# Position bias at block distances 2, 4 and 8 as one shape over summed spike blocks, in a spiking attention and expert kernel

## The reference, cut

```python
Q, K, V = (lif(layer_norm(query @ W.T + b, g, beta), 1.0) for each)   # spikes, 16 heads of 16
hamming = q_sum + swapaxes(k_sum) - 2.0 * qk
attn = Dh - hamming + log_pe_bias(N, N)      # max(ceil(log2((N-1) / (|i-j|+1))), 0)
out = lif(einsum('bhlm,bhmd->bhld', attn * scale, V), 0.5)
out = lif(layer_norm(out @ Wo.T + bo, go, betao), 1.0)
x = x + out + experts(xn)
```

## Time and profile before

| | |
|---|---|
| median of 3 runs | 443.77 us (443.08 to 443.96) |
| the profiled execution | 444.79 us, its span 442.9 us |
| busy | PE 378.5 (85%), DVE 273.0 (62%), ACT 232.5 (52%), POOL 214.5 (48%) |
| L1300 bias matmuls | 114, busy 380 ns each (pipelined) |
| L699 and L692 on POOL | 16 of 1332 ns and 11 of 1314 ns |
| y_tok loads | 8 of 1024 KB, 14.1 us to landing |

### The profile page before, as it was taken

How to read it: one execution, slowest core, us unless ns; L and a number is a source line. 1 busy time by engine, 2 the same in 40 slices (tenths; PEclk the granted TensorE clock), 3 DMA queues, 4 the chain that set the end, 5 groups by cost and what they waited for, 6 DMA issues and landing times.

```text
span 442.9 us, 9338 instructions
## 1 busy us (share of the span) xinstructions
PE 378.5 (85%) x2521; PEld 306.0 (69%) x2522; DVE 273.0 (62%) x774; ACT 232.5 (52%) x752; POOL 214.5 (48%) x213
## 2 busy tenths in 40 slices
PE   5388958999999508999999999999999998999840
PEld 1223657999999506778888888888888875666630
DVE  5796899777778505454445545444554434479994
ACT  1436835888888504544455455445445434466650
POOL 5215336777777750333333333333333332489993
PEclk9796979999999956999999999999999999999995
DMA  8880063424222231533334334333334413982222
GB/s 256 257 285 1 10 228 101 174 91 150 95 101 103 95 109 48 169 118 122 119 125 124 119 119 130 120 122 126 121 119 121 115 61 109 382 319 96 95 73 95
DMA packets 40108, 58.93 MB, mean 133 GB/s; under 512 B 5974, under 2 KB 27606, under 8 KB 40088
## 3 DMA queue, kind: packets, MB, share of 16 engines
q1 hardware_dynamic: 31392, 38.53, 27.6%
q0 software_dynamic: 6848, 18.70, 11.6%
q10 hardware_dynamic: 1848, 1.47, 1.1%
HBM read 35.79 MB, written 22.89 MB: 132 GB/s over the span
## 4 chain that ended last, share of the span: by engine, by line
PE 41%; POOL 26%; issue 13%; DMA 6%; DVE 5%; ACT 4%; SPq 3%; DVEq 0%; POOLq 0%; ACTq 0%
POOL slot_x L658 14%; PE bank L1085 12%; PE bank L1087 11%; PE bank L1086 11%; POOL xres L699 4%; POOL xres L692 3%; SPq L309 3%; PE bank L1212 3%; PE bank L1228 3%; DMA ew_f<-experts 2%; DMA vec_d<-two_col 2%; DVE exT_l L910 2%; POOL slot_x L665 2%; ACT gact L519 2%; DMA ex<-slot_x 1%
## 5 line engine op out<-in xcount | busy, mean ns | idle before, releaser
L673 POOL DMA_INDIRECT slot_y<-ey,dest x71 | 68.5, 965 | 139.7 <-ACT ey L535 111.4
L973 DVE TENSOR_TENSOR hid<-gact,bank 128x256 f32<-128x256 f32 x71 | 29.9, 421 | 77.6 <-ACT gact L519 77.6
L658 POOL DMA_INDIRECT slot_x<-xn,pos x64 | 64.7, 1011 | 25.6 <-issue 19.2
L1085 PE MATMUL bank<-ew,exT_h 128*128 x142 | 63.6, 448 | 5.3 <-DVE exT_l L910 5.2
L519 ACT ACTIVATE gact<-bank 128x256 f32<-128x256 f32 x71 | 27.4, 386 | 65.7 <-PE bank L1087 65.7
L1087 PE MATMUL bank<-ew,exT_l 128*128 x142 | 56.9, 401 | 0.0
L1086 PE MATMUL bank<-ew,exT_h 128*128 x142 | 56.8, 400 | 0.0
L1085 PE MATMUL bank<-w_h,xT_h 128*128 128x256 f32 x192 | 54.3, 283 | 0.0
L1087 PE MATMUL bank<-w_h,xT_l 128*128 128x256 f32 x192 | 54.1, 282 | 0.0
L1086 PE MATMUL bank<-w_l,xT_h 128*128 128x256 f32 x192 | 54.1, 282 | 0.0
L1085 PE MATMUL bank<-ew,hidT_h 128*128 x142 | 45.7, 322 | 1.0 <-DVE hidT_l L977 1.0
(11 more groups left out here) (183 smaller groups left out, 967.4 us busy)
## 6 DMA issues: line engine op xcount, KB each, us to landing
ex<-slot_x SPq DMA_DIRECT2D x71, 129.0 KB, 2.0
y_tok<-slot_y SPq DMA_DIRECT2D x8, 1024.0 KB, 14.1
xres<-x SPq DMA_DIRECT2D x16, 256.0 KB, 2.7
out<-xres SPq DMA_DIRECT2D x16, 256.0 KB, 2.1
xn<-x SPq DMA_DIRECT2D x6, 512.0 KB, 11.7
ew_f<-experts SPq DMA_DIRECT2D x1, 2560.0 KB, 10.1
ew_f<-experts SPq DMA_DIRECT2D x1, 2048.0 KB, 10.3
slot_y<-ey,dest POOLq DMA_INDIRECT x71, 2.4
```

The source lines that it names most:

```text
L658: pool.indirect_dma_start(slot_x, bass.IndirectOffsetOnAxis(ap=pos[:, k, t:t + 1], axis=0), xn[:, t, :], None).then_inc(s["scattered"], 16)
L673: pool.indirect_dma_start(slot_y, bass.IndirectOffsetOnAxis(ap=dest[:, m % 4:m % 4 + 1], axis=0), ey[:, m % 4, :], None).then_inc(y_out[m ...
L973: v.tensor_tensor(hid[:, m % 2, :], gact[:, m % 2, :], h_ps[m % 2][:, F:2 * F], ALU.mult).then_inc(s["hid_done"], 1)
L1085: mm(dst, a_h, b_h, start=first, stop=False)
```

## The change

OFFSETS, the distances with a matmul and a table of their own, shrink to 0, 1 and -1. For distances 2, 4 and 8 to one side the tables differ by a constant only. So the spikes of the three blocks are summed first, one matmul takes the common shape (UP for one side, DOWN for the other) times the sum, and the constants go to the far matmul's map. DVE makes the sums: `pair_v[a]` = block a + block a+2 for 14 values of a inside the expert loop, and `triple_v` = a pair and a single, one for each block a in the last stage, two slots. (The pair a+2 with a+4, and a+8; or on the other side a-4 with a-2, and a-8.) A side with two blocks takes a pair, with one block the spikes.

With it: output spikes `spk` become 16 bit and lie over `qT`, whose rows the same block has used. kv's correction has a place of its own, `less`. The first eight blocks of x (`xres_a`) are loaded in the expert loop, over `xn`, beside the pairs; the other eight (`xres_b`) behind the first two quarters of `y_tok`, at the end of the experts' weights. DVE waits for the scatter before its first pair.

```diff
-OFFSETS = [0, 1, -1, 2, -2, 4, -4, 8, -8]
+OFFSETS = [0, 1, -1]
+STEPS = [2, 4, 8]
+UP, DOWN = len(OFFSETS), len(OFFSETS) + 1
+PAIRS = NB - 2
+EARLY_RES = NB // 2
...
+        put = place_in(r_x)
+        xres_a = put("xres_a", [P, EARLY_RES, B, D])
+        pair_v = put("pair_v", [P, PAIRS * B * D], BF16)
+        triple_v = put("triple_v", [P, 2, B * D], BF16)
...
+        xres_b = put("xres_b", [P, NB - EARLY_RES, B, D])
+        less = put("less", [P, B * KC, P])
...
+        spk = place_in(r_q)("spk", [P, NB, B, D], BF16)
...
-            with sp.Fori(0, QUADS - 2) as i:
-                sp.dma_start(xres[:, bass.ds(i * B, B), :], x_pairs[:, bass.ds(i, 1), :, :].rearrange("p a b d -> p (a b) d")).then_inc(s["xres_in"], 16)
+            with sp.Fori(0, EARLY_RES) as i:
+                sp.dma_start(entry(xres_a, i), x_pairs[:, bass.ds(i, 1), :, :].rearrange("p a b d -> p (a b) d")).then_inc(s["xres_in"], 16)
+                for u in range(4):
+                    load_tile(i * 4 + (8 + u), u)
+            with sp.Fori(EARLY_RES, QUADS - 2) as i:
                 for u in range(4):
                     load_tile(i * 4 + (8 + u), u)
...
+                if c in (1, 2):
+                    half = (NB - EARLY_RES) // 2
+                    lo = (c - 1) * half
+                    for b in range(B):
+                        sp.dma_start(xres_b[:, lo:lo + half, b, :], x_pairs[:, EARLY_RES + lo:EARLY_RES + lo + half, b, :]).then_inc(s["xres_late"], 16)
...
                 if a == 0:
-                    pool.wait_ge(s["xres_in"], 16 * NB)
+                    pool.wait_ge(s["xres_in"], 16 * EARLY_RES)
+                if a >= EARLY_RES and a % 4 == 0:
+                    pool.wait_ge(s["xres_late"], 16 * B * (1 + (a - EARLY_RES) // 4))
...
+            def add_pair(a):
+
+                v.tensor_tensor(cut(pair_v, a * B * D, B * D), cut(v_spk, a * B * D, B * D), cut(v_spk, (a + 2) * B * D, B * D),
+                                ALU.add).then_inc(s["pair_set"], 1)
+
+            dve.wait_ge(s["spk_done"], G3 * NT)
+            dve.wait_ge(s["scattered"], 16 * TOPK * NT)
+            with dve.Fori(1, PAIRS + 1) as i:
+                for u in range(4):
+                    expert(i * 4 + u, 4 + u, i)
+                    if u == 1:
+                        add_pair(i - 1)
+            with dve.Fori(PAIRS + 1, QUADS) as i:
                 for u in range(4):
                     expert(i * 4 + u, 4 + u, i)
...
+            def add_triple(a):
+
+                if a == 0:
+                    dve.wait_ge(s["pair_set"], PAIRS)
+                if a >= 2:
+                    dve.wait_ge(s["s_done"], a - 1)
+                pair, single = (a + 2, a + 8) if a + 8 < NB else (a - 4, a - 8)
+                v.tensor_tensor(triple_v[:, a % 2, :], pair_v[:, pair * B * D:(pair + 1) * B * D],
+                                v_spk[:, single * B * D:(single + 1) * B * D], ALU.add).then_inc(s["triple_set"], 1)
...
+            add_triple(0)
+            add_triple(1)
             for a in range(NB + 2):
                 if a < NB:
                     out_spike(a)
+                if a + 2 < NB:
+                    add_triple(a + 2)
                 if a >= 2:
                     out_variance(a - 2)
...
+                if a == 0:
+                    pe.wait_ge(s["pair_set"], PAIRS)
+                pe.wait_ge(s["triple_set"], a + 1)
+                for way, shape in ((1, UP), (-1, DOWN)):
+                    if 0 <= a + 2 * way < NB:
+                        mm(dst[:, :], toep_s[:, shape, :], v_sum(a, way), start=False, stop=False, skip_group_check=True)
                 mm(dst[:, :], far_s[:, a * P:(a + 1) * P], far_v[:, :], start=False, stop=False, skip_group_check=True)
```

More of the change, by code:

```diff
@@ L131, in spiking_moe @@
         xn = place_in(r_x)("xn", [P, NT, ROW])
-        xres = place_in(r_x)("xres", [P, NT, D])
+        put = place_in(r_x)
+        xres_a = put("xres_a", [P, EARLY_RES, B, D])
+        pair_v = put("pair_v", [P, PAIRS * B * D], BF16)
+        triple_v = put("triple_v", [P, 2, B * D], BF16)
+        assert ends[r_x] == max(ends[r_x], r_x + NT * ROW * 4)
         r_w = ends[r_x]
@@ L213, in spiking_moe @@
         exT_l = put("exT_l", [P, 2, KC, P], F32R)
-        toep_s = put("toep_s", [P, len(OFFSETS), P], BF16)
+        toep_s = put("toep_s", [P, len(OFFSETS) + 2, P], BF16)
         far_s = put("far_s", [P, NB * P], BF16)
@@ L256, in spiking_moe, with xres @@
         y_in = [sem(f"y_in{c}") for c in range(YCH)]
+        def xres(a):
+            return xres_a[:, a, :, :] if a < EARLY_RES else xres_b[:, a - EARLY_RES, :, :]
         def num(i):
@@ L372, in _ @@
                     sp.wait_ge(s["late_done"], a - LATE + 1)
[L373 removed]
+                sp.dma_start(out_pairs[:, a], xres(a)).then_inc(s["out_done"], 16)
             sp.wait_ge(s["out_done"], 16 * NB)
@@ L697, in finish @@
                     pool.wait_ge(s["spk_added"], a + 1)
-                both = xres[:, a * B:(a + 1) * B, :]
+                else:
+                    pool.wait_ge(s["xres_late"], 16 * 2 * B)
+                both = xres(a)
                 g.tensor_tensor(both, both, y_tok[:, a, :, 0, :], ALU.add).then_inc(s["fin_done"], 1)
@@ L1017, in _ @@
             dve.wait_ge(s["half_summed"], 1)
-            half = spk[:, 0, :, :].rearrange("p b d -> p (b d)").rearrange("p (g k) -> p g k", k=P)
-            v.tensor_tensor(half, half_ps[:, :].rearrange("p (g k) -> p g k", k=P), heads, ALU.mult).then_inc(s["kv_less"], 1)
+            dve.wait_ge(s["up_done"], SLOT_TILES)
+            dve.wait_ge(s["down_done"], SLOT_TILES)
+            v.tensor_tensor(less[:, :, :], half_ps[:, :].rearrange("p (g k) -> p g k", k=P), heads, ALU.mult).then_inc(s["kv_less"], 1)
             dve.wait_ge(s["kv_less"], 1)
-            v.tensor_tensor(kv[:, :, :], kv[:, :, :], half, ALU.add).then_inc(s["kv_fixed"], 1)
+            v.tensor_tensor(kv[:, :, :], kv[:, :, :], less[:, :, :], ALU.add).then_inc(s["kv_fixed"], 1)
             dve.wait_ge(s["gate_exp"], 1)
@@ L1293, in _, with v_sum @@
             pe.wait_ge(s["toep_in"], 32)
+            def v_sum(a, way):
+                inside = [a + way * k for k in STEPS if 0 <= a + way * k < NB]
+                if len(inside) == 3:
+                    return triple_v[:, a % 2, :]
+                lo = min(inside) * B * D
+                return pair_v[:, lo:lo + B * D] if len(inside) == 2 else v_spk[:, lo:lo + B * D]
             def attend(a, near):
@@ L1360, in position_tables @@
         toep[:, n, :] = blocks[a, a + k].T
+    above = {}
+    for way, shape in ((1, UP), (-1, DOWN)):
+        a = 0 if way > 0 else NB - 1
+        base = {k: blocks[a, a + way * k].min() for k in STEPS}
+        toep[:, shape, :] = (blocks[a, a + way * STEPS[0]] - base[STEPS[0]]).T
+        for k in STEPS:
+            assert (blocks[a, a + way * k] - base[k] == toep[:, shape, :].T).all()
+            above[way * k] = base[k]
     edges = [P - 1, 0, 1, P - 2]
@@ L1370, in position_tables @@
         for m in range(NB):
-            if m not in near:
+            if m - a in above:
+                far_map[m, a, :] = above[m - a]
+            elif m not in near:
                 level = np.median(blocks[a, m])
```

12 lines of the change are left out of this document (4 added, 8 removed).

## The result

The changed kernel takes 444.10 us (median of 20 runs, 441.64 to 446.22), the kernel before, run beside it, 442.62 (20 runs, 441.55 to 443.96). The ratio is 1.0030, 95% interval 1.0016 to 1.0043: the change makes the kernel slower, by 0.7 to 1.9 us. Forecast was 444.0, so the level is met almost to the tenth. The step is not: +0.2 was forecast from a base of 443.77, and +1.3 to +1.5 was measured from a base that these runs put 1.15 lower.

What follows compares the result with a forecast made beforehand. In the last stage PE was taken as the bound first, then DVE and POOL. Stage +0.45 and loop -0.3 gave +0.2 on a median of 443.77, so 444.0 us, range 442.0 to 446.5 for 8 in 10.

Steps and rivals of the forecast that it cites:

- What bounds the stage: Last stage: with 74 bias matmuls for 114, PE sets a 2.99 us pace to rstd 4, then DVE and POOL bound.
- The start: Start of the last stage: PE waits for triple 0 behind DVE's gates, so rstd 0 comes 0.98 us later.
- rival (b): Start of the last stage: PE's standstill makes its granted clock fall to half, +1.9 us, 445.9; chance 0.2.
- The price of a triple: On DVE in the last stage: one 128x512 sum in 16 bit takes 0.42 us, 0.34 to the next start.
- The rounds: Last stage: net gain 1.3 us by rstd 5, then triples on the path to rstd cost 1.74 up to rstd 11.
- 16-bit spikes: POOL's add_spikes in the last stage: reading 16-bit spikes taken as 0, between -2.2 and +0.7 us.
- Behind rstd 11: End of the last stage: nothing of the change lies on the path there, 0.
- The loop: Expert loop: the smaller bias table shortens a wait for rows, -0.3 us; fourteen pairs fit DVE's idle time, 0.
- x behind the experts: Loads between the y_tok loads: later y_tok data delays nothing, taken as 0, at most 5.4 us if cover is gone.
- (a): Last stage: a triple's time follows its elements, 0.69 us, net +2.4, 446.2; chance 0.13.
- (e): Other contention, such as pairs blocked in the expert loop, 446 us and more; chance 0.07.

Runs made afterwards that it cites:

- filled at both places: The changed kernel plus ten matmuls nobody reads before PE's wait for triple 0 and three per block from 8 on: 442.35 us, ratio 0.9984 to the kernel before.
- unread matmuls: Matmuls whose results nobody reads, three per block from 8 on, added to three variants of the changed kernel: ratios 0.9984, 0.9943 and 0.9968 to the kernel before.
- triples made twice: The changed kernel with each triple from 2 on computed twice, first into a place nobody reads: 447.23 us, ratio 1.0094 to the kernel before.
- triples behind veps: The changed kernel with each round's triple after veps on DVE, not before: ratio 1.0068 to the kernel before; 1.0010 with triples 0 and 1 also moved ahead.
- triples 0 and 1 early: The changed kernel with triples 0 and 1 made right behind DVE's last expert operation, ahead of kv's correction and the gates: ratio 0.9965 to the kernel before.
- triples spread: The changed kernel with a slot per triple, 0 and 1 before the stage, fourteen in its first six rounds: 440.26 us, ratio 0.9931 to the kernel before.
- the fill at the start alone: The changed kernel with ten matmuls nobody reads ahead of PE's wait for triple 0, none later: ratio 0.9998 to the kernel before.

## Why the prediction was right and where it was wrong

- **What bounds the stage.** Right. 74 bias matmuls instead of 114 give a pace of 3.00 for the forecast 2.99, it holds for four intervals, and then POOL and DVE set the pace.
- **The start.** The wait was sized right, 1.09 for 0.98. The step that failed is the one behind it, "The clock" in rival (b): held at 0.2 with +1.9, it happened in the profiled run and costs 1.63. It was held back by "before the gap PE is busier than it was at 150". That is so in the traces (busy 1.62 of the 2.00 us up to 367 in the changed kernel, 0.73 of those up to 151.2 in the kernel before), and the clock fell all the same.
- **The price of a triple.** Right: 0.41 in quiet for 0.42. The Trainium skill, page "VectorE: DVE Perf Modes", section "The perf-mode tier table", has tensor_tensor at twice the rate when its operands are 16-bit in SBUF; the trace agrees, 0.41 for the triple and 0.69 for kv's correction with its mixed operands.
- **The rounds.** 3.68, 4.33 and 4.77 for the forecast 3.78, 4.44 and 4.75. The triples cost 1.93 from rstd 5 to 11 where 1.74 was worked out, the rest of it in the two rounds with two finishes (0.31 and 0.35 for 0.2). The gain by rstd 5 is 2.30 from rstd 0 on, as worked out.
- **16-bit spikes.** A mis-sized term: taken at 0, it is -0.67. "Nothing in the trace ties POOL's time to bytes" was true of the trace, and I took it for a reason; the middle of the bounds, -0.75, would have been nearer.
- **Behind rstd 11.** "The rest moves as it is" failed. After the change PE runs out of bias matmuls earlier, stands 2.34 for o_spk, and its clock fell during blocks 14 and 15, 0.59, of which other intervals give back 0.15 (3.99 for 4.11 from rstd 11 to 12, as with 16-bit spikes alone). I had counted PE's spare time as worth nothing; here it cost something.
- **The loop.** From POOL's first send of rows to its fifth it takes 11.74 for 12.09: 0.35 less for the forecast 0.3, PE's one wait for rows being 0.66 for 1.04. That the smaller table is the reason is argued, no run has it alone. The fourteen pairs cost nothing visible: DVE is idle 0.97 before a `hid`, 0.64 where a pair stands ahead of it, and the rounds stay at 10.70. About 0.3 more that the loop's traces differ by has no cause that I can name. The first send comes 1.05 earlier, in front of anything that the change touches, with the clock at 0.65 instead of 0.52 from 166 to 174. Kernels with the change differ in this among themselves (back at 1.00 before 172 here, only behind 173 when filled at both places), so it is no gain of the change.
- **x behind the experts.** Right, 0.

The sum of the stage is +0.45 by the forecast and +2.12 by the trace. Between the two lie 1.63 and 0.59 for the clock, 0.1 for the wait and 0.2 for the triples, less 0.67 for the 16-bit spikes and 0.15 at the end. With the loop's -0.35 that is +1.8. The profiled pair itself differs by 0.33, for the first send came 1.05 earlier and 0.3 of the loop is unexplained; the runs have 0.7 to 1.9. That the forecast time is met is chance: the base was 1.15 too high and the change 1.1 to 1.3 too small. In the chances, (a), (b) and (e) alone make 0.40, not 0.39 with a little of the forecast.

How often the clock falls in runs without a profile is open. At the start it did in two of three traces that have the full wait of 2.61, and behind rstd 11 in five of the seven without unread matmuls there.

## What to carry to other kernels

Work that replaces matmuls must not be put in front of a waiting PE, nor between two operations on the path of the engine that becomes the bound. Sums that depend on nothing in the stage are cheapest where PE still sets the pace, and a kilobyte per partition for each buys that freedom: the same 74 matmuls and 16 triples gave 1.0030 in one order and 0.9931 in the other. Before moving a small operation into "free" time of an engine that shares SBUF with POOL, look at what stands in the quiet stretch beside POOL's short operations, since something is pushed out of it.

## What the runs showed of the hardware

- PE that stood for 2.61 us, after 4.00 us in which it was busy 2.98 (363 to 367 in the changed kernel), was granted 1.2 GHz in two executions (0.79 in the microsecond from 369 and 0.50 behind it; with the triples made twice 0.83 from 368) and 2.4 GHz in a third (triples behind veps, 1.00 all through). In the changed kernel it lasted until 373, with PE busy all the time from 369.63 on.
- Late in the stage, where PE stood 2.34 for o_spk, the clock fell in the changed kernel and with triples 0 and 1 early. It fell too beside a standstill of 1.99 (triples spread), of 3.35 and 3.27 (the two kernels with triples behind veps) and of 1.77 (triples made twice, at 419). After the same 2.34 it stayed with the fill at the start alone. Where PE stood 1.80 (the kernel before), 1.69 or 1.33 (with three more matmuls a block) it stayed. So falls and no falls lie side by side at the same length, and I can't say what decides the single case. The count is plainer: seven of seven traces with the lighter load fell at least once between rstd 5 and 14, none of six with the load of before or three unread matmuls a block from 8 on. In the changed kernel the fall from 410 to 413 cost nothing and the one from 424 cost 0.59.
- POOL's tensor_tensor of 128x512 takes 1.17 with one 16-bit input beside one of 4 bytes, and 1.29 with both of 4 bytes.
- A DVE tensor_tensor in 16 bit takes 1.16 to 1.17 when it is issued into a POOL tensor operation (1.50 into the later of two), for 0.41 in quiet; so it ends 0.28 after POOL's (400.20 + 1.16 against the first finish, begun at 399.80), whatever its own length. The Trainium skill, page "GPSIMD Engine Reference", section "Specifications", says that DVE instructions with two SBUF inputs contend with POOL; the trace agrees (1.16 for 0.41). veps, with one input of two elements per partition, waits likewise (1.25 for 0.15).
